# A fused four-layer kernel: new tables of the order in which side work is laid between the main pieces

## The chip, the cores and the metric

The kernel runs on one core of a Trainium2 chip. It has a matrix engine (TensorE, PE), a vector engine (VectorE, DVE), a scalar engine (ScalarE, ACT), a general engine (GpSimd, POOL) and a queue engine (SyncE, SP) that here issues the DMA transfers. Each works through its own list of instructions in order and meets the others through semaphores. The metric is the device time of one execution in microseconds; of several, the median.

## The reference

The input x is 8 images of 256 channels of 64 x 64 pixels, fp32. Four layers follow one another, each on the group-normalised value with a residual:

```python
def _gn(v, G=32, eps=1e-5): ...            # groups of 8 channels
# layer 0: three gates, mixed by weights from a 1-D convolution
b3 = x * sigmoid(bn(conv7x7([x.max(axis=1), x.mean(axis=1)])))
# b1, b2: the same with the channel axis swapped with H, with W
pooled = ((b1 + b2 + b3) / 3.0).mean(axis=(2, 3))
wts = softmax(conv1d(pooled, w1d), axis=1)
y0 = (wts * stack([b1, b2, b3])).sum(axis=1)
# layer 1: 3x3 convolution, 256 -> 256, with
w = a[0] * weight + sum(a[i + 1] * _cir_project(weight, b) for b in (2, 4, 8, 16))
# layer 2: the mean of a wavelet low band, then squeeze and excite
w = sigmoid(relu(mean(dwt2_ll(x)) @ W1.T) @ W2.T);  y2 = x * w
# layer 3: attention in shifted 8x8 windows, 8 heads
attn = softmax(q @ k.T * dh ** -0.5 + bias + mask);  y3 = (attn @ v) @ w_o + b_o
```

## The kernel before

**Main line.** One image after another goes through the same list of main pieces, FRONT: norm0a to norm0c (normalisation, with statistics gathered before), reduce0 to reduce15 (maxima and means over channels, transposed on PE), zpool, hwconv, hwgate, hwrows, band0 to band3, bandcopy, bandturn, hwmean0 to hwmean7 (the three 7x7 convolutions as products with band tables, and their gates), logits, mix, mixturn, gate0 to gate17 (layer 0's sum), norm1a to norm1c, lift0 to lift3 (normalisation and the transform of the convolution's input), conv0.0 to conv23.1 (24 accumulations in two halves, matmuls of 128x512) and convend. In the last image the attention remains to be done.

**Side streams.** Beside the main line each engine has streams of other work. A letter stands for the next step of a stream:

- POOL: R row sums over channels of the next image (lines 960 to 971), D differences and W weighed rows for layers 1 and 2, E the power in the excitation (line 910), N normalised probabilities (line 915), O heads (line 930), Y setup. Line 834 is the main line's power that gives the reciprocal root of a variance.
- DVE: C and U statistics and maxima of the next image (lines 1720, 1735, 1742), V row sums of layer 2 (lines 1706, 1709), B input transform, J the sums that join layer 1 to its residual, E excitation, K token remainders, S scores with bias and their maxima (lines 1836, 1847), T totals, A additions (line 1864), Y setup (line 1275 sums the circulant blocks of the weights). Line 1423 writes the convolution's input; line 1547 writes s, which PE needs before the bands.
- PE: Q a fill of qkv or output projection (lines 2141, 2148, 2157), S the score pairs (line 2173, tiles of 32 x 64), T turns (line 2183), W the products with the values (line 2201, tiles of 64 x 32), E, Y. S and W use small tiles; everything else uses the whole array.
- ACT: K token rows, Q evacuations of the fills (line 1189 writes vv), X exponentials, T, O, H, E, Y. Line 1080 writes g_raw for the reduces.
- SP: L loads and S stores of attention rows, Z stores of the image to scratch, F fetches of the next image, G the band tables again (its third transfer is line 681), Y setup.

The attention of image n thus runs beside the main line of image n + 1, and the statistics of image n + 1 beside the convolution of image n.

**Order.** Four tables set where each letter stands. FIRST is for image 0 and TURN for images 1 to 7: after the main piece that is the key, the letters of the value are played. AHEAD says how many letters of TURN have been played in image 0 already and are left out once, in image 1. LAST_ROWS is what follows after the last main piece. All engines read their own table; nothing else orders the steps. Per image the tables hold the same letters for SP (25), POOL (92), ACT (160), DVE (162) and PE (150).

## Time and profile before

| | us |
|---|---|
| median of 3 runs | 2744.55 |
| lowest and highest run | 2733.57, 2748.24 |
| profiled execution, span | 2740.3 |
| PE busy | 2332.0 |
| DVE busy | 2165.5 |
| ACT busy | 1538.2 |
| POOL busy | 1436.9 |
| a steady image (one of images 2 to 6), length | 310.7 |
| the same, PE busy and DVE busy | 285.56, 256.34 |
| from the last convolution matmul to the end | 211.0 |

The profiled execution lies between the runs. The busy times of the engines overlap, so their sum says nothing; what counts is where PE stands still and which engine it then waits for. A steady image repeats itself within about 3 us. A timeline row gives its start, its duration, engine, line, operation, what is written and read, a count, and in brackets the time for which the engine had nothing before it and whose result ended that.

### The profile page before, as it was taken

The numbers are of one execution on the slowest core, as the hardware profiler recorded it, in microseconds if no ns is written. First come the engines' busy times: TensorE is split into PE (matmuls) and PEld (weight loads), VectorE is DVE, ScalarE is ACT, GpSimd is POOL, SyncE is SP. The second block draws the span as 40 slices with busy tenths as digits, with TensorE's granted clock in tenths as the row PEclk, the third lists the DMA queues.
The fourth block names the chain that finished last, engine by engine and source line by source line (L and its number), as shares of the span: only waits on it lengthen the run. The fifth ranks groups of instructions, "written<-read, shape, count | busy, mean of one in ns | idle before, by whom it ended". The sixth has DMA issues, their size and how long they took to land.

```text
span 2740.3 us, 67622 instructions
## 1 busy us (share of the span) xinstructions
PE 2332.0 (85%) x27766; PEld 1395.9 (51%) x27766; DVE 2165.5 (79%) x3697; ACT 1538.2 (56%) x3566; POOL 1436.9 (52%) x1150
## 2 busy tenths in 40 slices
PE   0457738899899989899898989899898999899887
PEld 0433326455654556554664556555664556545454
DVE  6877957878887798878887798869887788867655
ACT  1222126654775566754775566754766567655665
POOL 3324562456734574465834575465834575465455
PEclk9878969999999999999999999999999989999999
DMA  5400400115111331115111241105110241101121
GB/s 155 127 3 16 158 19 18 32 47 171 33 33 47 98 105 33 33 35 174 40 33 39 83 128 33 32 32 161 57 33 25 79 146 33 33 32 57 54 63 41
DMA packets 125428, 176.20 MB, mean 64 GB/s; under 512 B 72496, under 2 KB 114240, under 8 KB 115520
## 3 DMA queue, kind: packets, MB, share of 16 engines
q1 hardware_dynamic: 125120, 171.88, 20.0%
q8 instruction: 220, 3.60, 0.5%
q14 instruction: 88, 0.72, 0.1%
HBM read 98.95 MB, written 72.86 MB: 63 GB/s over the span
## 4 chain that ended last, share of the span: by engine, by line
PE 54%; DVE 23%; ACT 8%; issue 6%; POOL 4%; DMA 2%; SPq 2%; DVEq 0%; POOLq 0%; ACTq 0%
PE F L2082 18%; PE QP L2141 9%; PE QP L2148 4%; PE SP L2173 4%; PE F L1979 3%; PE O L2201 3%; PE QP L2157 3%; PE PTR L2183 2%; PE F L1955 2%; DVE g_raw L1423 2%; DVE xs L1836 2%; DVE mx L1847 1%; ACT xs L1201 1%; POOL tmp L960 1%; DVE sums L1855 1%
## 5 line engine op out<-in xcount | busy, mean ns | idle before, releaser
L2082 PE MATMUL F<-g_raw,cw_hi 128*128 128x512 f16 x2304 | 701.1, 386 | 20.7 <-DVE g_raw L1423 6.5
L1201 ACT ACTIVATE xs<-xs,mx 128x64 f32<-128x64 f32 x1792 | 445.7, 334 | 123.8 <-DVE mx L1847 123.8
L915 POOL TENSOR_TENSOR xs<-xs,rec 128x512 f32<-128x512 f32 x256 | 287.9, 1136 | 432.5 <-DVE rec L1857 428.3
L2082 PE MATMUL F<-g_raw,cw_lo 128*128 128x512 f16 x1152 | 443.8, 385 | 0.0
L2082 PEld LDWEIGHTS F<-g_raw,cw_hi 128*128 128x128 f16 x2304 | 224.2, 99 | 286.5 <-issue 17.8
L1208 ACT ACTIVATE prt<-PTR 128x512 f32<-128x512 f32 x256 | 151.0, 590 | 216.8 <-PE PTR L2183 191.0
L900 POOL TENSOR_TENSOR tmp<-X,uw 128x512 f32<-128x512 f32 x128 | 165.3, 1303 | 164.0 <-DVE y L1709 83.0
L1836 DVE TENSOR_TENSOR xs<-SP,bias 128x1024 f32<-128x1024 f32 (+2 forms) x192 | 159.7, 859 | 100.0 <-issue 54.2
L1423 DVE SCALAR_TENSOR_TENSOR g_raw<-l0c,gn,g_raw 128x512 f16<-128x512 f32 x192 | 171.6, 936 | 72.2 <-ACT g_raw L1140 36.9
L930 POOL TENSOR_TENSOR ot_lo<-ot,ot_hi 128x512 f16<-128x512 f32 x128 | 149.1, 1187 | 145.8 <-ACT ot_hi L1222 132.7
L2141 PE MATMUL QP<-tok_hi,qkv_hi 128*128 128x512 f16 x470 | 180.1, 383 | 43.4 <-ACT qq L1182 17.3
L1855 DVE TENSOR_REDUCE sums<-xs 128x16 f32<-128x1024 f32 x128 | 155.2, 1212 | 72.2 <-ACT xs L1201 46.0
L1182 ACT ACTIVATE qq<-QP,q_bias,q_scale 128x512 f32<-128x512 f32 x118 | 91.6, 776 | 202.7 <-PE QP L2141 202.5
L1979 PE MATMUL F<-ident,g_raw 128*128 128x129 f32 x1024 | 153.1, 296 | 45.6 <-DVE Z L1528 22.7
L2082 PEld LDWEIGHTS F<-g_raw,cw_lo 128*128 128x128 f16 x1152 | 113.9, 99 | 142.2 <-issue 6.5
L2141 PE MATMUL QP<-tok_hi,qkv_lo 128*128 128x512 f16 x470 | 179.6, 382 | 0.0
L2141 PE MATMUL QP<-tok_lo,qkv_hi 128*128 128x512 f16 x470 | 179.3, 381 | 0.0
L2201 PE MATMUL O<-prt,vv 64*32 64x64 f32 x8192 | 162.0, 222 | 8.1 <-ACT prt L1208 7.5
L1979 PEld LDWEIGHTS F<-ident,g_raw 128*128 128x128 f32 x1024 | 135.0, 203 | 65.3 <-DVE Z L1528 33.5
L1847 DVE TENSOR_REDUCE mx<-xs 128x16 f32<-128x1024 f32 x128 | 156.2, 1220 | 14.4 <-DVE xs L1836 0.9
L2183 PE MATMUL PTR<-ident,xs 128*128 128x128 f32 x1024 | 158.7, 278 | 6.5 <-ACT prt L1208 4.2
L2173 PE MATMUL SP<-kk,qq 32*64 32x64 f32 x8192 | 155.1, 225 | 5.2 <-ACT kk L1185 4.2
(331 smaller groups left out, 5586.4 us busy)
## 6 DMA issues: line engine op xcount, KB each, us to landing
scratch_x<-X SPq DMA_DIRECT2D x32, 1024.0 KB, 5.8
...
l0c<-scratch_t SPq DMA_DIRECT2D x8, 576.0 KB, 13.7
```

The lines of the kernel that those rows point to most:

```text
L915: G.tensor_tensor(keyed(sc[:, u % 4, :]), keyed(sc[:, u % 4, :]), rec[:, u % 4, :].unsqueeze(2).to_broadcast([P, 8, TOK]), ALU.mult).then_ ...
L1201: last = S.activation(keys, keys, ACT.Exp, bias=mx[:, u % 4, i:i + 1])
L1423: V.scalar_tensor_tensor(vin[:, slot(half, comp), 1, t, :, 1:1 + W], rows_view(src[:, t, :]), g_r[:, t:t + 1], vin[:, slot(half, comp), 0, ...
L1836: return V.tensor_tensor(windows(sc[:, buf:buf + 2, :])[:, :, w0:w1_, :], windows(SP[:, :, :])[:, :, w0:w1_, :], bias[:, kind, :, :, :].re ...
L1847: V.tensor_reduce(mx[:, buf:buf + 2, :].rearrange("p a k -> p (a k)"), sc[:, buf:buf + 2, :].rearrange("p a (k m) -> p (a k) m", m=TOK), A ...
L1855: seq.link(V.tensor_reduce(both(sums), sc[:, buf:buf + 2, :].rearrange("p a (k m) -> p (a k) m", m=TOK), AX.X, ALU.add))
L1979: last = T.matmul(turned_pair(j)[:, t, :], Gn[:, t, P * j:P * j + P], ident_mean[:, :], start=True, stop=True)
L2082: last = T.matmul(F[:, n % 2, :], wgt[:, ci, C3 * comp + dx, P * co:P * co + P], win[which], start=(ci == 0 and dx == 0 and j == 0), stop= ...
L2141: last = T.matmul(out_bank, wgt[:, ci, P * oc:P * oc + P], tk[:, ci, :], start=(j == 0), stop=(j == 5))
L2173: last = T.matmul(SP[TOK * h2:TOK * h2 + TOK, hs, 256 * cg + TOK * w:256 * cg + TOK * w + TOK], qq[rows, cg, win], kk[rows, cg, win], star ...
L2183: last = T.transpose(PTR[:, P * b:P * b + P], sc[:, u % 4, P * b:P * b + P], ident[:, :])
L2201: last = T.matmul(O[DH * (h % 4):DH * (h % 4) + DH, par, cols:cols + TOK], vv[rows, pair, DH * h:DH * h + DH], prt[rows, u % 2, P * b + TO ...
```

## The change

The four tables are laid out anew; no other line is touched. All letters of an image are still played as often as before over the whole program; POOL plays fewer R and one E fewer in image 0 and so more of them in image 1, DVE two A more. SP's G for image 1 is played in image 0, as before; for a later image it is now played in that image's own norm0a, and no longer in the convolution ahead of it. Some entries, before and after (in the changed kernel every line behind the tables has a number lower by 3):

```diff
 FIRST = {
-    "SP": {"norm0a": "Y", "reduce9": "YY", "hwmean1": "Y", "hwmean7": "Z", "mix": "F", "gate7": "Z", "conv1.1": "F",
-        "conv3.1": "F", "conv6.1": "G", "conv12.0": "ZZ", "conv21.1": "F", "conv23.1": "L"},
...
+    "SP": {"load": "Y", "reduce4": "Y", "reduce12": "Y", "gate2": "YZ", "gate3": "Z", "gate7": "F", "gate16": "F",
+        "lift2": "F", "conv5.0": "Z", "conv9.1": "F", "conv13.1": "Z", "conv15.0": "L", "conv19.0": "G"},
...
-    "DVE": {"load": "CCUCYCCCYCCUCYCYUYYUCYUCCCCCYY", "norm0b": "UY", "norm0c": "YY", "reduce0": "Y",
...
+    "DVE": {"load": "CCYCCCCCCCCCUCCUCCYCYYYYYYY", "norm0b": "UYY", "norm0c": "YY", "reduce0": "Y", "reduce1": "Y",
...
-    "PE": {"reduce10": "YY", "hwconv": "Y", "hwmean0": "Y", "hwmean5": "Y", "gate5": "Y", "gate8": "Y",
...
+    "PE": {"zpool": "Y", "hwconv": "Y", "hwrows": "Y", "band1": "Y", "hwmean5": "Y", "gate1": "Y", "norm1b": "Y",
...
 TURN = {
...
-    "PE": {"norm0b": "Q", "norm0c": "QT", "reduce0": "TQ", "reduce1": "QW", "reduce3": "Q", "reduce4": "T",
...
-        "gate17": "QQQT", "norm1a": "QT", "lift0": "SWT", "lift1": "WQ", "lift3": "STWWQ", "conv0.1": "Q",
...
+    "PE": {"norm0c": "QQTQ", "reduce0": "T", "reduce2": "Q", "reduce3": "WW", "reduce4": "Q", "reduce5": "TQ",
...
+        "gate15": "QQQT", "norm1b": "W", "lift0": "T", "lift1": "QW", "lift2": "T", "lift3": "QSTWW",
+        "conv0.1": "SQQ", "conv1.0": "Q", "conv2.1": "T", "conv6.0": "Q", "conv6.1": "T", "conv7.0": "Q",
...
```

In DVE's table of TURN, "norm1c": "S" is gone and "conv4.0" is "KSB"; "norm0b": "ET", "norm0c": "AKKUA" become "norm0a": "E", "norm0b": "T", "norm0c": "AKKAU"; convend changes from JJJVVVVCVVVVVEECEECESCECESE to JJJVVVVVVVVVECECEECESECESE; conv12 to conv17 hold less and conv18.1 holds VVCSJUJCCCJVCSV. In PE's, "conv17.1" is QTWSQTWSWW. In SP's, G goes from conv6.0 to the next image's norm0a.

The first place is PE in a steady image, from lift3 to the convolution (lines 2082 and 2079 are the convolution's matmuls, F the accumulators, QP the fills' bank, SP and O the scores' and the products'). Before:

```order
L2173 MATMUL SP<-kk,qq 64x64 x32
L2183 MATMUL PTR<-ident,xs 128x128 x4
L2201 MATMUL O<-prt,vv 32x64 x32
L2148 MATMUL QP<-qkv_hi,tok_hi 128x256
L2148 MATMUL QP<-qkv_hi,tok_lo 128x256
L2148 MATMUL QP<-qkv_lo,tok_hi 128x256
...
L2082 MATMUL F<-g_raw,cw_hi 128x512 x2
L2082 MATMUL F<-g_raw,cw_lo 128x512
```

And after:

```order
L2170 MATMUL SP<-kk,qq 64x64 x32
L2180 MATMUL PTR<-ident,xs 128x128 x4
L2198 MATMUL O<-prt,vv 32x64 x32
L2079 MATMUL F<-g_raw,cw_hi 128x512 x2
L2079 MATMUL F<-g_raw,cw_lo 128x512
...
L2170 MATMUL SP<-kk,qq 64x64 x32
L2145 MATMUL QP<-qkv_hi,tok_hi 128x256
```

The fill that stood ahead of the first convolution matmuls, and a pair of scores with it, stand behind the first two halves.

The second place is DVE while image 0 is loaded (line 1275 before and 1272 after sum the weights' blocks; stats and Z are the image's statistics and maxima). Before, the stretch from the first statistics to norm0a:

```order
L1720 BN_STATS stats<-X 128x6 x2
L1735 TENSOR_REDUCE Z<-X 128x16
L1720 BN_STATS stats<-X 128x6
L1275 TENSOR_TENSOR cw_lo<-xs 128x128x9 x2
...
L1275 TENSOR_TENSOR cw_lo<-cw_lo,xs 128x2x63
L1735 TENSOR_REDUCE Z<-X 128x16
L1720 BN_STATS stats<-X 128x6 x5
L1275 TENSOR_TENSOR cw_lo<-cw_lo,xs 128x2x72 x2
...
L1399 BN_AGGR mv<-stats 128x2 x2
```

And after:

```order
L1717 BN_STATS stats<-X 128x6 x9
L1732 TENSOR_REDUCE Z<-X 128x16
...
L1272 TENSOR_TENSOR cw_lo<-xs 128x128x9 x2
...
L1272 TENSOR_TENSOR cw_lo<-cw_lo,xs 128x2x63
L1272 TENSOR_TENSOR cw_lo<-cw_lo,xs 128x2x72 x2
...
L1396 BN_AGGR mv<-stats 128x2 x2
```

Within the weights' sums no statistics or maxima are left; all of the statistics stand ahead of them.

The third place is POOL at the passage from image 0 to image 1 (tmp and Z are the row sums, part the excitation's operand, gn the normalisation's). Before:

```order
L960 TENSOR_TENSOR tmp<-X 128x512
L960 TENSOR_TENSOR tmp<-l0c 128x512
L910 TENSOR_TENSOR part<-part,neg_half 128x2
L960 TENSOR_TENSOR tmp<-tmp,X 128x512
L960 TENSOR_TENSOR tmp<-tmp,l0c 128x512
...
L971 TENSOR_TENSOR Z<-tmp 128x64
L974 MEMSET tmp 128x1024
L834 TENSOR_TENSOR gn<-gn,neg_half 128x2
```

And after:

```order
L957 TENSOR_TENSOR tmp<-X 128x512
L957 TENSOR_TENSOR tmp<-l0c 128x512
L907 TENSOR_TENSOR part<-part,neg_half 128x2
L831 TENSOR_TENSOR gn<-gn,neg_half 128x2
L912 TENSOR_TENSOR xs<-xs,rec 128x512 x2
L957 TENSOR_TENSOR tmp<-tmp,X 128x512
L957 TENSOR_TENSOR tmp<-tmp,l0c 128x512
```

The rest of the row sums now stands behind the reciprocal root of norm0.

## Rows read from the trace of the kernel before

**Rows 1.** The page: span, each engine's busy time, chain that ended last by engine.

```profile
span 2740.3 us, 67622 instructions
...
PE 2332.0 (85%) x27766; PEld 1395.9 (51%) x27766; DVE 2165.5 (79%) x3697; ACT 1538.2 (56%) x3566; POOL 1436.9 (52%) x1150
...
PE 54%; DVE 23%; ACT 8%; issue 6%; POOL 4%; DMA 2%; SPq 2%; DVEq 0%; POOLq 0%; ACTq 0%
```

**Rows 2.** Table of windows, steady image: length, busy (instructions) per engine, clock, DMA share, GB/s.

```profile
976.10:999.90 23.80, 17.31 (x338) 11.83 (x336) 20.96 (x57) 13.46 (x32) 16.75 (x13) 1.00 0.44 135
...
1138.30:1154.50 16.20, 12.04 (x304) 9.18 (x303) 12.84 (x22) 10.21 (x19) 4.84 (x4) 0.89 0.01 2
...
1219.00:1258.20 39.20, 39.20 (x378) 20.91 (x377) 33.17 (x41) 19.04 (x40) 17.48 (x13) 1.00 0.23 68
1258.20:1286.80 28.60, 27.42 (x191) 13.15 (x190) 27.21 (x41) 15.67 (x45) 16.46 (x14) 1.00 0.75 240
sum 310.70, PE 285.56 PEld 171.25 DVE 256.34 ACT 194.27 POOL 172.47; mean PE 25.96 PEld 15.57 DVE 23.30 ACT 17.66 POOL 15.68
```

**Rows 3.** Timeline of PE within a convolution: start, duration, line, operation, count.

```profile
889.78 0.65 PE L2201 MATMUL O<-prt,vv 64*32 64x64 f32 x32
890.36 0.66 PE L2183 MATMUL PTR<-ident,xs 128*128 128x128 f32 x4
...
903.45 0.99 PE L2201 MATMUL O<-prt,vv 64*32 64x64 f32 x64
904.37 0.61 PE L2082 MATMUL F<-g_raw,cw_hi 128*128 128x512 f16 x2
```

**Rows 4.** Timeline of all engines before the convolution (brackets: idle before, releaser).

```profile
1142.71 1.23 DVE L1836 TENSOR_TENSOR xs<-SP,bias 128x1024 f32<-128x1024 f32 x1 [0.55 <-PE SP L2173]
...
1144.04 1.22 DVE L1847 TENSOR_REDUCE mx<-xs 128x16 f32<-128x1024 f32 x1
...
1147.35 1.42 DVE L1423 SCALAR_TENSOR_TENSOR g_raw<-l0c,gn,g_raw 128x512 f16<-128x512 f32 x2 [0.95 <-ACT g_raw L1062]
...
1150.17 2.35 POOL L814 TENSOR_TENSOR l0c<-l0c 128x1024 f32<-128x1024 f32 x1 [7.27 <-DVE l0c L1409]
1150.95 2.78 DVE L1423 SCALAR_TENSOR_TENSOR g_raw<-l0c,gn,g_raw 128x512 f16<-128x512 f32 x2 [0.86 <-ACT g_raw L1062]
1151.37 0.57 ACT L1189 ACTIVATE vv<-QP 128x512 f32<-128x512 f32 x1
...
1151.99 0.39 PE L2148 MATMUL QP<-qkv_hi,tok_hi 128*128 128x256 f16 x1 [2.97 <-ACT vv L1189]
```

**Rows 5.** The page's group of the line that writes the convolution's input.

```profile
L1423 DVE SCALAR_TENSOR_TENSOR g_raw<-l0c,gn,g_raw 128x512 f16<-128x512 f32 x192 | 171.6, 936 | 72.2 <-ACT g_raw L1140 36.9
```

**Rows 6.** Timeline at the head of a steady image, ACT and PE.

```profile
1005.40 2.36 ACT L1080 ACTIVATE g_raw<-X,gn 128x1024 f32<-128x1024 f32 x2
...
1007.82 1.16 PE L1979 MATMUL F<-ident,g_raw 128*128 128x129 f32 x8 [0.85 <-ACT g_raw L1080]
```

**Rows 7.** Timeline of image 0, DVE during loading.

```profile
31.31 3.96 DVE L1275 TENSOR_TENSOR cw_lo<-xs 128x1152 f32<-128x1152 f32 x4 [11.19 <-DMA xs<-in_w_conv]
...
41.28 1.86 DVE L1742 TENSOR_REDUCE Z<-X 128x32 f32<-128x1024 f32 x1
...
53.81 3.06 DVE L1720 BATCH_NORM_STATS2 stats<-X 128x6 f32<-128x512 f32 x5
```

**Rows 8.** Timeline of image 0, PE in the reduces and before the band.

```profile
114.54 1.52 PE L1920 MATMUL SP<-ident,xs 128*128 128x128 f32 x6 [6.14 <-DMA xs<-scratch_w]
...
142.57 0.39 PE L2000 MATMUL F<-ident,s 128*32 128x128 f32 x1 [12.38 <-DVE s L1547]
```

**Rows 9.** Timeline of DVE between image 0 and image 1.

```profile
364.95 0.16 DVE L1767 SCALAR_TENSOR_TENSOR part<-F,part 128x2 f32<-128x2 f32 x1 [12.33 <-POOL part L910]
...
389.07 0.16 DVE L1450 SCALAR_TENSOR_TENSOR gn<-F,gn 128x2 f32<-128x2 f32 x1 [2.98 <-POOL gn L834]
```

**Rows 10.** Timeline of SP's queue in a steady image.

```profile
949.73 9.82 SPq L681 DMA_DIRECT2D l0c<-scratch_t  x1
```

More of the change, by code:

```diff
@@ L52 @@
 FIRST = {
[20 rows of a table removed]
-        "conv23.1": "UVV", "convend": "JJVJVCCVCVCVVCUVVVCEUUUCEEUECECUEUUEUUCCECUCE"},
-    "PE": {"reduce10": "YY", "hwconv": "Y", "hwmean0": "Y", "hwmean5": "Y", "gate5": "Y", "gate8": "Y",
-        "conv19.1": "Y", "conv23.1": "EEEEEE"},
[21 rows of a table added]
+        "convend": "JAJJCVVVVVVVVYUCUUEUCUEUCCCUUCEEECUCCECCACUEUUEE"},
+    "PE": {"zpool": "Y", "hwconv": "Y", "hwrows": "Y", "band1": "Y", "hwmean5": "Y", "gate1": "Y", "norm1b": "Y",
+        "conv1.0": "Y", "conv23.1": "EE", "convend": "EEEE"},
@@ L76 @@
 }
 TURN = {
[35 rows of a table removed]
-        "convend": "JJJVVVVCVVVVVEECEECESCECESE"},
[11 rows of a table removed]
-        "conv23.1": "TQTWWTQWQTEWE", "convend": "QEESEQSEQ"},
[14 rows of a table added]
+        "logits": "TQTX", "mix": "XQOQ", "mixturn": "KKX", "gate2": "T", "gate3": "K", "gate5": "KQXQT",
[16 rows of a table added]
+        "conv23.0": "VCK", "convend": "JJJVVVVVVVVVECECEECESECESE"},
+    "PE": {"norm0c": "QQTQ", "reduce0": "T", "reduce2": "Q", "reduce3": "WW", "reduce4": "Q", "reduce5": "TQ",
+        "reduce6": "ST", "reduce7": "WWSQ", "reduce8": "Q", "reduce10": "Q", "reduce13": "T", "reduce14": "Q",
+        "reduce15": "QTWQ", "hwconv": "QTWQT", "hwgate": "WQWS", "hwrows": "QSQ", "bandcopy": "Q", "bandturn": "T",
[8 rows of a table added]
+        "convend": "QTWTQTWWEWEQEESEQSEQ"},
@@ L127 @@
 }
-AHEAD = {"SP": {}, "POOL": {"R": 28, "E": 1, "N": 4, "O": 1}, "ACT": {"X": 2, "T": 4, "O": 1}, "DVE": {"U": 13, "E": 1, "T": 2, "A": 2}, "PE": {"Q": 2, "T": 4, "W": 4}}
+AHEAD = {"SP": {"G": 1}, "POOL": {"N": 4, "O": 1, "R": 22}, "ACT": {"O": 1, "T": 4, "X": 2}, "DVE": {"A": 4, "E": 1, "T": 2, "U": 13}, "PE": {"Q": 2, "T": 4, "W": 4}}
 LAST_ROWS = {
-    "SP": "LSLSLSLSLSLSLSSSL",
-    "POOL": "ENNNNXOXXNNXNXXNOXNNXNNXXONXXNNNXXXNOXNNNXXNOXNXNNXXOXNNXNNXXXOXNNNNXXXNXONNNO",
-    "ACT": ("KKXXQTQQKKTQTTXOKKXKQQQXQXTKTTTXOXKKKTXQXQTKQQTTOKXXKTXQXQQQKTTKXTXOXKKXQTQQQKTKTTXXOKTKQXXQTQKQTTOK"
-            "KXKXKXQQTXQQTKTXTXOKKKTQXXQQKQTTXTXXOTXTTTO"),
-    "DVE": "EATKAKTSSPPKKAATTSPSPTKAKATSSPKTKPAATSSTPPKAKATSTPPKSKAATSPSKAPKATTSSPPTKKAATSSTPTPAAASTA",
-    "PE": ("QQTQQQTQQWTSQTWSWWQQQQQQTTSWQQWTSTWWQQTQQQTQTWWSQTWWSQQQQTQQQTWSTTSWQWWQQQTQQQQTSTWWTQWWQSTQQWQQTQQW"
-            "TSWTSWQQQQQQQTQQTSTWWTSWWQQQQTQQTQWSTWTSWWQQTQQTWTWTWWQQ"),
+    "SP": "LSGLSLSLSLSLSLSSLS",
+    "POOL": "ENNNNOXXXNXNNNXXONXXNNNXOXXXNNNNXXONXXNNNXXONNXXNNXOXNXNXNNXXONXXNNNXXXNXNONNO",
+    "ACT": ("KKXXKQTKTQQQTTOKKXXQQQXXTQTKTKKTXXOKXTKXQQKTQQTTOKKXXXKQXQTQTQKTTOXXKKXQXTKKQQQTTTXOXKKTXXQQKTQQTTOX"
+          "KKKXQQXXTQQTKKTKTOKXXQQXXTQQTTKXTXOTXXKTTTO"),
+    "DVE": "EAKKATTSPSKPKAATTSKPTPSKAATSPSKPKAATTSSPTKPKAATSSPTKPKAATSSPPAKKTATSPKSPKTAATSSTPPTATAASA",
+    "PE": ("QQQQTQTQTWWSWTQWSQQQQQQQTQTSWTQWTWWSQQTQQQTQTWWSWTQWSQQQQQQTQTWWTSTWWSQQQQTQQQTQWSTWWTSWQQQQTQTQQQWW"
+          "TSTWWSQQQQQQQTQQTWSTQWTWWSQQQQTQQTSWTSTWQWWQTWTQWTQTWWQQ"),
```

115 rows, old and new, of tables (FIRST, TURN) are left out of this document.

## The prediction

> **What bounds the kernel now.** I read the page first. TensorE (PE) is busy for 85% of the span and is 54% of the chain that ended last; VectorE (DVE) is 79% busy and 23% of that chain; GpSimd (POOL) has 4% of it [rows 1]. So PE sets the time, DVE is next, and an edit counts only where PE stands still. The table of windows says where that is. A steady image takes 310.70 us with PE busy for 285.56 of it and DVE for 256.34 [rows 2], so PE idles 25.1 us an image. None of that lies in conv12 to conv17 (39.20 busy of 39.20). The 23.8 us between the last convolution matmul and the next norm0 hold 6.5 us of it, with DVE busy for 20.96 there, and the 16.2 us of norm1 and lift before the convolution hold 4.2, at a granted clock of 0.89 [rows 2]. The rest is small stops in the other stages. A shuffle inside the convolution is covered by PE; one at its two borders is not. Image 0 and the passage from image 0 to 1 have waits of their own, up to 12 us each [rows 7 to 9].
>
> The sum is made against the profiled span of 2740.3 us [rows 1], which is 4 us under the median of the runs; a saving in it is taken off the median, 2744.55, one to one.
>
> **Image 0.** Loading: DVE waits 11.19 us for the convolution's weights and then does, between its weight sums, seven pieces C and three U of the image's statistics [rows 7]. The new order puts the C in front of the wait, and of U two; the third goes behind norm0. Five C take 3.06 us, so seven take 4.3; U take 1.86, 1.86 and about 1.2, so 4.9. norm0 should begin 9.2 us earlier. PE then stops for 6.14 us inside the reduces, for a weight transfer needed by a setup step, and 12.38 us before the band, for DVE's s [rows 8]. The setup step moves behind the reduces, so the first stop goes. The second is a chain: s needs POOL's row sums, and these now stand 16 before the clearing of hwgate and 4 behind it, where there were 10 and 10. It can't give back more than the two waits and the load together less what DVE still owes: the setup pieces are not fewer, only later, and DVE is nearly the whole time busy here. From above 9.2 and a part of the 12.38, some 14; from below 0, if the weight chain, which has to be through before conv0, sets the end. I take 11, near the load term, since that is the one with an idle wait in front.
>
> **Image 0 to 1.** With no attention rows to fill it, this passage is a chain DVE, POOL, DVE. DVE idles 12.33 us for POOL's power in the excitation, and 2.98 us for POOL's rsqrt in norm0 [rows 9]. Before, POOL works at row sums in front of each. Now the last six of them stand behind the rsqrt: of the 2.98 some 0.7 is the operation itself, so 2.3 is gained. DVE's eight V, which release these row sums, are no longer mixed with five C and a U (3.1 + 1.2 by [rows 7]); an addition and one C now precede them (0.7 + 0.6), which leaves 3.0. Before the first power stands one row sum more (about 0.4 with its share of the small ones), before the second one fewer (1.3). -2.3 - 3.0 + 0.4 - 1.3 = -6.2; and the fetch that DVE waits for stands earlier on SP. From -2 (POOL's rate is the limit and the V gain nothing) to -10. I take **-6.2**.
>
> **A steady image, seven times.** Four edits lie outside the convolution's cover.
> - *norm1 and lift.* Before conv0, DVE has scores in its way (1.23 and 1.22) and PE has a fill that waits 2.97 us for ACT's vv, although conv0's own input was written by 1148.8 (1147.35 + 1.42) [rows 4]. After, one S and that fill are behind conv0, and DVE's S of norm1c is gone from there. Conv0 comes between 1.4 us earlier (what the letters take off DVE less what ACT puts back) and 5 (the whole wait and the slow restart of PE behind it). I take 2.5, most of the 2.97 that is seen, since the next convolution pieces need the second L1423, at 1150.95, too.
> - *norm0.* The first reduce waits 0.85 us for ACT's g_raw, two of 2.36 us together [rows 6]; a fill more stands before it on PE, which fills that wait, and an addition comes before a maximum on DVE. -0.8.
> - *The tail.* One C fewer (0.6) between the V. -0.6, or worse by up to 1 where the C placed behind the first E meets a fetch that is not down.
> - *Small and whole tiles.* A lone W begins 0.58 us before the next matmul; two in a row take 0.92, 0.46 each [rows 3]. So a change costs 0.12 us. I counted the changes in the new order: 481 against 530 in the program, 61 against 68 in each of these images. 7 x 0.12 = 0.8, of which I take 0.7, the changes in stages where PE waits anyway giving nothing.
>
> Against these stand a scores piece and a K more where PE already waits for DVE in the mix (+0.5), and the block that goes into conv18 and 19: DVE has about 6 us more in conv18 to conv22 and 7.5 less in conv12 to 17. I book +1.5 for its lateness, and price the bad case below. -2.5 - 0.8 - 0.6 - 0.7 + 0.5 + 1.5 = **-2.6** an image, seven times **-18**. From +2 (no gain at conv0, the block as booked) to -5.
>
> The port: line L1423 takes 1.42 us for two when alone and 2.78 beside POOL's L814 [rows 4]; DVE's maxima at 1.86 [rows 7] read from one place only and are not in that state. The Trainium skill (SBUF — State Buffer, section Who interferes with whom) says that a DVE operation with two SBUF inputs contends with a GpSimd one that reads SBUF, while a tensor_reduce never contends. By that rule a table that keeps POOL away from DVE gains on two-input lines alone, and if all of that counted the sum would be rival 4's. The trace agrees, with the 2.78. What all of L1423 loses is bounded by its group: 171.6 us for 192 [rows 5], against 192 x 0.71, is 35 us in the program, 4.4 an image. Nearly all of it lies in the convolution, where DVE has room (33.17 of 39.20 [rows 2]) and PE doesn't wait. So I book nothing for it; the one on the path, the 1.36 of [rows 4], still has L814 beside it.
>
> SP: the band tables' transfer, 9.82 us of SP's queue [rows 10], goes from the convolution to norm0 of the next image. There it delays a load of attention rows, not a fetch, and has the whole reduce stage until hwconv needs it; nothing booked.
>
> **The ending** has 8 tile changes or so fewer and otherwise the same latency-bound pattern: **-1**, from -6 to +5, since the order within it is a new one all through.
>
> **Sum.** -11 - 6.2 - 18 - 1 = -36.2: 2744.55 - 36.2 = **2708**.
>
> **The rivals.**
> 1. *The steady image doesn't move.* The convolution eats what is gained at its head, because DVE gets to conv18 no sooner and the tail is bound by DVE (20.96 of 23.8). For it: DVE is busy 256 of 310 and nothing is removed from it. Against: the 2.97 is a wait of PE. Then only -11 - 6.2 - 1 are left, and some of it: 2722 to 2735, about 2727. Chance 0.20.
> 2. *Slower: DVE is late at conv18 to conv23.* In these 28.60 us DVE is busy 27.21 [rows 2]. With 6 more it would need 33.3, 4.7 more than PE's own pace, and the accumulators' emptying would hold PE. It decides when the 6 us don't fit into the block of attention work that PE now has before conv18 (some 7.7 us of it by the durations of its letters). Seven images at 4.7, with the other gains of an image kept at 2, less image 0's and the passage's, is +19 - 18.2, about even; if the held PE also falls to the lower clock at the restart, as the fill at 1151.99 did [rows 4], 2.5 more each: +17. 2745 to 2775, **2762**. Chance 0.14.
> 3. *Image 0's gain is lost* to the weight chain: 2719. Chance 0.12.
> 4. *The ports count for more*: the shorter L1423 bring DVE sooner to the tail, 4.4 an image at most, half of it is -15: 2692, down to 2677. Chance 0.08.
>
> **How the numbers follow.** The forecast case (2695 to 2722) has 0.44; 0.02 is left for none of these. A measurement of this kernel tells about 0.5%, 13.7 us, from no change. Faster by more than that (under 2731): the forecast, rivals 3 and 4, and a third of rival 1: 0.44 + 0.12 + 0.08 + 0.06 = 0.70. Same: the rest of rival 1 and the even end of rival 2, 0.18. Slower: 0.12. The range is 2680 to 2748: it takes in the forecast, rivals 1 and 3 and most of 4, and leaves out most of rival 2.
>
> **What would show it.** Right: norm0 of image 0 some 9 us earlier, by the loading term; the stop of 6.14 us gone; POOL's rsqrt of image 1 directly behind a power; conv0 of a steady image 14 us instead of 16.2 after norm1's begin, with no wait for vv in front; some 308 us an image. Wrong: DVE waits for nothing in conv18 to 23 while PE waits for its gather (rival 2); the band's wait for s still over 10 us (rival 3); PE waits before hwconv for the tables.

## The result

| | us |
|---|---|
| before, median of 4 runs | 2742.92 |
| changed kernel, median of 4 runs | 2648.03 (2641.66 to 2652.97) |
| ratio, 95% interval | 0.9655 (0.9632 to 0.9679) |
| profiled execution of the changed kernel, span | 2651.2 |

The kernel is 3.45% faster, 95 us, where 36 were predicted: the direction was right, the size was 2.6 times too small, and the time lies below the predicted range.

The page of the changed kernel, the lines that answer to [rows 1]:

```profile
span 2651.2 us, 67608 instructions
...
PE 2304.1 (87%) x27766; PEld 1386.2 (52%) x27766; DVE 2186.5 (82%) x3697; ACT 1535.1 (58%) x3566; POOL 1441.2 (54%) x1150
...
PE 48%; DVE 17%; POOL 11%; ACT 7%; issue 5%; DMA 0%; DVEq 0%; SPq 0%; POOLq 0%; ACTq 0%
```

PE is busy for 28 us less and DVE for 21 us more. So DVE did not become quicker; it spends more time, in places where nobody waits for it. PE runs the same 27766 matmuls; the mean clock that it was granted over the execution goes from 0.951 to 0.961. So of the 89 us between the two spans 61 are idle time of PE and 28 are work that it did in less time. In the chain that ended last POOL goes from 4% to 11%.

The two profiled executions cut at the same eight borders (start to norm0, to conv0, to the last convolution matmul of image 0, to norm0 of image 1, to norm0 of image 2, to norm0 of image 7, to its last convolution matmul, to the end), in windows: length, busy time of PE, PEld, DVE, ACT and POOL, clock, DMA share, GB/s. Of before the sixth and the last:

```profile
689.20:2242.70 1553.50, 1434.24 (x17325) 859.34 (x17325) 1286.92 (x2175) 970.84 (x2342) 868.00 (x685) 0.97 0.21 66
...
2529.30:2740.30 211.00, 173.59 (x3162) 108.95 (x3160) 118.66 (x182) 131.44 (x233) 104.13 (x95) 0.97 0.18 54
```

And after, six of the eight:

```profile
52.40:202.90 150.50, 73.40 (x406) 53.91 (x407) 133.64 (x283) 41.02 (x75) 42.59 (x36) 0.80 0.22 60
202.90:309.50 106.60, 98.44 (x433) 42.45 (x434) 89.78 (x121) 22.58 (x35) 58.25 (x40) 0.97 0.17 60
309.50:355.40 45.90, 4.01 (x18) 3.11 (x16) 40.63 (x83) 0.56 (x2) 39.77 (x33) 0.55 0.46 149
355.40:654.00 298.60, 275.76 (x3297) 166.89 (x3297) 235.99 (x408) 185.20 (x444) 142.31 (x108) 0.97 0.16 51
654.00:2170.10 1516.10, 1415.89 (x17325) 851.85 (x17325) 1303.63 (x2175) 968.38 (x2341) 875.61 (x686) 0.98 0.22 68
...
2450.00:2651.20 201.20, 171.45 (x3162) 109.34 (x3160) 118.32 (x183) 130.55 (x232) 101.77 (x94) 0.98 0.18 54
```

| stretch | before | after | difference | predicted |
|---|---|---|---|---|
| start to conv0 of image 0 | 217.6 | 202.9 | -14.7 | -11 |
| convolution of image 0 | 112.8 | 106.6 | -6.2 | 0 |
| to norm0 of image 1 | 53.6 | 45.9 | -7.7 | -6.2 |
| seven images (305.2 + 1553.5 + 286.6 before) | 2145.3 | 2094.6 | -50.7 | -18 |
| the ending | 211.0 | 201.2 | -9.8 | -1 |
| sum | 2740.3 | 2651.2 | -89.1 | -36.2 |

The prediction's term for the passage reaches past the border at norm0, to the rsqrt behind it, which comes 2.1 us earlier after that border (5.07 and 2.93 us behind it, before and after): by its own borders the passage gained 9.8 and the seven images 48.6.

More than half of what was missed lies in the seven images. In them PE is busy for 22.0 us less (1978.8 and 1956.8) and idle for 28.7 less. One of them, beginning with the tail of the image ahead, stage by stage (the windows of after that answer to [rows 2], with norm0, the reduces, two stages from there to norm1, and the first convolution pieces). Of before, those that [rows 2] does not have:

```profile
999.90:1007.80 7.90, 5.46 (x20) 2.46 (x20) 6.44 (x20) 7.52 (x18) 5.63 (x7) 0.78 0.00 0
1007.80:1045.90 38.10, 35.28 (x466) 27.20 (x467) 34.13 (x58) 28.63 (x66) 33.19 (x30) 1.00 0.11 33
...
1072.50:1100.40 27.90, 25.14 (x364) 17.05 (x364) 23.00 (x65) 17.40 (x45) 6.60 (x6) 0.88 0.13 39
1100.40:1138.30 37.90, 33.71 (x409) 18.57 (x410) 35.18 (x54) 27.67 (x74) 18.32 (x14) 1.00 0.19 58
...
1154.50:1183.00 28.50, 28.37 (x127) 12.58 (x125) 18.24 (x25) 18.60 (x51) 15.96 (x11) 0.94 0.00 1
```

And after:

```profile
935.10:958.00 22.90, 17.13 (x339) 11.68 (x337) 20.75 (x55) 13.07 (x33) 15.83 (x12) 1.00 0.44 140
958.00:967.60 9.60, 8.04 (x26) 3.48 (x27) 7.00 (x21) 8.29 (x17) 9.13 (x11) 0.64 0.05 19
967.60:1003.30 35.70, 34.84 (x503) 28.02 (x502) 33.60 (x56) 28.23 (x66) 31.45 (x27) 1.00 0.42 130
...
1028.40:1056.80 28.40, 24.36 (x360) 16.51 (x361) 22.02 (x64) 16.47 (x44) 4.58 (x5) 0.88 0.13 38
1056.80:1094.00 37.20, 33.91 (x410) 18.20 (x409) 35.30 (x55) 28.47 (x75) 21.12 (x16) 1.00 0.19 59
1094.00:1104.10 10.10, 8.48 (x228) 6.39 (x226) 6.54 (x16) 6.04 (x12) 1.60 (x2) 1.00 0.01 2
1104.10:1135.00 30.90, 29.54 (x207) 14.00 (x200) 27.92 (x31) 21.13 (x54) 15.86 (x10) 1.00 0.12 35
...
1172.70:1211.10 38.40, 38.40 (x425) 20.36 (x423) 33.43 (x46) 16.50 (x40) 18.31 (x14) 1.00 0.34 111
1211.10:1238.40 27.30, 27.30 (x140) 12.83 (x133) 25.80 (x39) 15.68 (x43) 17.16 (x15) 1.00 0.25 78
sum 303.30, PE 283.48 PEld 170.58 DVE 260.13 ACT 193.62 POOL 174.71; mean PE 25.77 PEld 15.51 DVE 23.65 ACT 17.60 POOL 15.88
```

An image takes 303.3 us where it took 310.7. PE stands still for 19.8 us (303.30 - 283.48) instead of 25.1, and is busy for 2.1 less. Norm1 and lift fall from 16.2 to 10.1 us, with the clock at 1.00 and no longer at 0.89; the first six convolution pieces grow by 2.4, since a fill and a scores pair are now among them: 41.0 for both stages against 44.7. Of these 3.7 us only 1.3 are idle time; PE's busy time over both stages falls from 40.41 to 38.02, and its granted clock, 0.89 and 0.94 there before, is 1.00 in both. The rest is in small amounts: the reduces with norm0 45.3 against 46.0, conv18 to 23 27.3 against 28.6, the tail 22.9 against 23.8. The 28.6 holds a stop of 1.18 us of PE, for DVE's addition (line 1864), that the trace of before has in this one of the seven images only.

### The profile page after: what moved, and what is told of

Its sections match the earlier page's. It is cut to its first block, busy times and chain, and to the rows that moved or that the text cites. A ratio compares the mean times of both kernels' runs of the same rounds, so it can differ in the third digit from the quotient of the medians.

```text
span 2651.2 us, 67608 instructions
## 1 busy us (share of the span) xinstructions
PE 2304.1 (87%) x27766; PEld 1386.2 (52%) x27766; DVE 2186.5 (82%) x3697; ACT 1535.1 (58%) x3566; POOL 1441.2 (54%) x1150
## 4 chain that ended last, share of the span: by engine, by line
PE 48%; DVE 17%; POOL 11%; ACT 7%; issue 5%; DMA 0%; DVEq 0%; SPq 0%; POOLq 0%; ACTq 0%
PE F L2079 22%; PE QP L2138 6%; POOL tmp L957 5%; PE O L2198 3%; PE QP L2154 3%; PE SP L2170 3%; PE QP L2145 3%; PE PTR L2180 3%; ACT xs L1198 2%; DVE xs L1833 2%; DVE stats L1451 1%; POOL ot_lo L927 1%; DVE sums L1852 1%; POOL tmp L964 1%; DVE mx L1844 1%
## 5 line engine op out<-in xcount | busy, mean ns | idle before, releaser
L2079 PE MATMUL F<-g_raw,cw_hi 128*128 128x512 f16 x2304 | 693.5, 383 | 14.8 <-DVE X L1491 7.2
L1420 DVE SCALAR_TENSOR_TENSOR g_raw<-l0c,gn,g_raw 128x512 f16<-128x512 f32 x192 | 161.8, 885 | 59.0 <-ACT g_raw L1059 36.5
L2079 PEld LDWEIGHTS F<-g_raw,cw_lo 128*128 128x128 f16 x1152 | 112.8, 98 | 139.4 <-issue 1.4
L1182 ACT ACTIVATE kk<-QP,bq,gm 128x512 f32<-128x512 f32 x117 | 90.6, 774 | 161.3 <-PE QP L2138 161.3
```

What stands on the lines that cost most here:

```text
L2079: last = T.matmul(F[:, n % 2, :], wgt[:, ci, C3 * comp + dx, P * co:P * co + P], win[which], start=(ci == 0 and dx == 0 and j == 0), stop= ...
```

## The experiments

Three of them give each table alone, seven cut the one for images 1 to 7 into stretches or engines, and the others move single letters of it. All times are medians, with the ratio against the kernel before, measured beside it, and its 95% interval; the medians of before lay between 2742.5 and 2743.7.

### Each table alone

`e1_lastrows` takes the new LAST_ROWS, all else as before:

```diff
 LAST_ROWS = {
-    "POOL": "ENNNNXOXXNNXNXXNOXNNXNNXXONXXNNNXXXNOXNNNXXNOXNXNNXXOXNNXNNXXXOXNNNNXXXNXONNNO",
+    "POOL": "ENNNNOXXXNXNNNXXONXXNNNXOXXXNNNNXXONXXNNNXXONNXXNNXOXNXNXNNXXONXXNNNXXXNXNONNO",
...
```

> The kernel before with only the new LAST_ROWS (SP's string kept). The prediction's own term for the ending is -1 us: about 2742. The trace of the changed kernel has the stretch from the last convolution matmul to the end at 201.2 us against 211.0, so if the new order of the last rows does that by itself, -9.8: about 2733. A rival: the ending is shorter because the tail and the state in which it is entered are, then LAST_ROWS alone gives nothing.

Measured: 2735.47, ratio 0.9965 (0.9951 to 0.9978), -7.2. The ending's order is worth most of the 9.8 by itself; in this run's trace PE's last convolution matmul is 200.4 us from the end, as in the changed kernel, and in that of `e3_turns`, with the old LAST_ROWS, 213.3. The term was -1. `e2_firstimg` takes the new FIRST and AHEAD:

```diff
 FIRST = {
-    "DVE": {"load": "CCUCYCCCYCCUCYCYUYYUCYUCCCCCYY", "norm0b": "UY", "norm0c": "YY", "reduce0": "Y",
+    "DVE": {"load": "CCYCCCCCCCCCUCCUCCYCYYYYYYY", "norm0b": "UYY", "norm0c": "YY", "reduce0": "Y", "reduce1": "Y",
...
```

> The kernel before with only the new FIRST (and AHEAD, which belongs to it; TURN and LAST_ROWS as before). The prediction's terms: -11 for image 0 and -6.2 for the passage, so -17: about 2726. By the trace of the changed kernel norm0 of image 1 comes 28.6 us earlier (355.4 against 384.0), 6.2 of it in image 0's convolution, for which the prediction had nothing: about 2714. If the late row sums that are then left to image 1 cost it something, between the two.

Measured: 2714.31, ratio 0.9889 (0.9866 to 0.9913), -28.4: all that the trace showed up to norm0 of image 1. `e3_turns` takes the new TURN:

```diff
 TURN = {
-    "SP": {"reduce4": "L", "reduce8": "S", "hwconv": "L", "band1": "S", "band3": "L", "mix": "S", "gate3": "L",
+    "SP": {"norm0a": "G", "reduce7": "L", "reduce10": "SL", "band3": "S", "mix": "L", "gate5": "S", "norm1a": "L",
...
```

> The kernel before with only the new TURN (FIRST and LAST_ROWS as before; SP's extra G is accounted for in AHEAD and LAST_ROWS). The prediction's term is 7 x -2.6 = -18: 2725. By the traces a steady image takes 303.3 to 303.7 us against 310.4 to 312, so -7.3 x 7 = -51 for the seven images: about 2692. If less than -40, part of what the traces show there comes in from image 0 and is not TURN's.

Measured: 2688.79, ratio 0.9793 (0.9767 to 0.9818), -53.9. The three add up to -89.5 of the 95: the tables hardly depend on one another, and each earned, within some 3 us, what its stretch of the trace shows.

### One letter of the sum's largest term

`e4_onefill`, on the kernel before:

```diff
 TURN["PE"]
-    "lift3": "STWWQ", "conv0.1": "Q",
+    "lift3": "STWW", "conv0.1": "QQ",
```

> The kernel before with one letter moved in TURN: the fill that waits 2.97 us for vv goes from lift3 (ahead of conv0) to conv0.1, on PE alone. The prediction takes 2.5 of this for each of seven images: -17.5, 2725. If PE's restart at the lower clock goes too (the fill in 2.5 us instead of 1.3, and the first convolution matmuls), up to -5 each: -35, 2708. If DVE's path to the second L1423 is what conv0 waits for in truth, the wait only moves into the convolution: 0 to -5.

Measured: 2741.86, ratio 0.9996 (0.9984 to 1.0009): nothing. Its timeline, PE and ACT behind the first convolution matmuls:

```profile
1150.97 0.57 ACT L1189 ACTIVATE vv<-QP 128x512 f32<-128x512 f32 x1
...
1154.83 2.00 ACT L1201 ACTIVATE xs<-xs,mx 128x64 f32<-128x64 f32 x8
...
1156.74 0.57 ACT L1189 ACTIVATE vv<-QP 128x512 f32<-128x512 f32 x1
...
1157.37 0.61 PE L2157 MATMUL QP<-ot_hi,wo_hi 128*128 128x512 f16 x1 [3.38 <-ACT vv L1189]
```

Conv0 does start earlier, 10.7 us behind norm1 instead of 16.2, and PE no longer waits ahead of it. But the fill now finds its bank full behind conv0: PE waits 3.38 us there instead of 2.97 ahead ([rows 4]), for the next vv, which stands behind eight exponentials on ACT. Norm1 to conv5 takes 44.1 us against 44.7. DVE's chain to conv0's input is not shortened by this move either: in the trace of before its second line 1423 begins 10.0 us behind line 1443 of the same norm1 (1150.95 and 1140.95), with the scores of norm1c between them; in the changed kernel, where these are gone, 7.9 us.

`g1_fillvv` takes these exponentials away from it as well:

```diff
 TURN["ACT"]
-    "lift2": "XQK",
+    "lift2": "QXK",
```

> The kernel before with two letters moved: the fill from lift3 to conv0.1 on PE (as in e4_onefill, which gave 0) and ACT's second evacuation of lift2 ahead of the exponentials. In e4_onefill's trace PE's wait of 2.97 us for vv became one of 3.38 us behind conv0, with eight exponentials (2.0 us) in front of vv on ACT. If ACT's order was what ate the gain: -2.0 an image, -14: about 2729. If DVE's chain ahead of conv1 holds it: the wait moves on once more, 0 to -4.

Measured: 2739.76, ratio 0.9985 (0.9972 to 0.9999), -4.0. Two waits of PE in `g1_fillvv`'s timeline:

```profile
1152.51 0.39 PE L2157 MATMUL QP<-ot_hi,wo_hi 128*128 128x512 f16 x1 [1.48 <-ACT vv L1189]
...
1158.37 0.61 PE L2157 MATMUL QP<-ot_hi,wo_hi 128*128 128x512 f16 x1 [2.44 <-DVE xs L1864]
```

The wait for vv is down to 1.48 us, and behind it is one of 2.44 for DVE's addition, line 1864, that was not there before. `h1_fillvvadd` was to take this next one away too:

```diff
 TURN["DVE"]
-    "lift1": "S", "conv0.0": "A",
+    "lift1": "S", "lift3": "A",
```

> As g1_fillvv (fill behind conv0, vv ahead of the exponentials), and DVE's addition from conv0.0 to lift3. In g1_fillvv's trace the wait for vv fell from 3.38 to 1.48 us, and a new one of 2.44 us stood behind it, for this addition, which waited behind two L1423 and an L1413 on DVE. If it is the next in the row and no more stand behind it: -2.4 an image, -17: 2723. If the addition now holds DVE up ahead of the convolution's input, as it has to wait for the fill: 0 or slower.

Measured: 2740.57, ratio 0.9985 (0.9975 to 0.9996), with the 1.48 and the 2.44 us as they were. It tells nothing of the addition: on DVE no step of the main line lies between lift3 and conv0.0, so every engine has the instructions of `g1_fillvv` in the same order, and the run is a repeat of it (-3.0 beside -4.0). Whether the addition is the last in the row stays open. `g2_head` keeps `g1_fillvv`'s letter of ACT, leaves the addition and moves the scores pieces, as the new tables do:

```diff
 TURN["PE"]
-    "lift3": "STWWQ", "conv0.1": "Q",
+    "lift3": "TWW", "conv0.1": "SQQ",
 TURN["DVE"]
-    "norm1c": "S", "conv4.0": "A",
+    "conv4.0": "SA",
```

> As g1_fillvv, and the scores piece of norm1c on DVE and its pair on PE go behind conv0 too, as in the new tables. If these four moves are the whole of what the new tables do at the head of the convolution (norm1 to conv5 from 44.7 to 41.1 us): -25, 2718. If the ACT letters of norm1a to norm1c, which this leaves as they were, are needed as well: about as g1_fillvv.

Measured: 2759.98, ratio 1.0066 (1.0044 to 1.0087): 16 us slower. With the scores gone from norm1c, DVE waits 2.73 us for ACT to pad the rows (line 1047), which still stands behind two of ACT's turns, and the scores' time is missing further on: PE waits 1.86 us for them behind conv0, then 0.69 for vv and 1.97 for the addition. So these moves, which the new tables make too, are a loss while ACT's letters of norm1 and what follows up to conv5 stand as they did.

The same letter the other way round, `f5_undofill` on the changed kernel, and the one wait left there, `f4_vv`:

```diff
 TURN["PE"]
-    "lift3": "QSTWW", "conv0.1": "SQQ",
+    "lift3": "QSTWWQ", "conv0.1": "SQ",
```

> The changed kernel with one fill back ahead of conv0 (the prediction's largest single term undone, in the new surroundings). The prediction's -2.5 an image undone: +17, 2666. If in the new order of ACT and DVE the fill would find vv ready: only the wait that the traces show, 0 to +1 an image, 2648 to 2655.

Measured: 2676.78, ratio 0.9769 (0.9745 to 0.9794): 29 us slower than the changed kernel, 4.1 an image. PE's row ahead of conv0:

```profile
1112.46 0.40 PE L2148 MATMUL QP<-qkv_hi,tok_hi 128*128 128x256 f16 x1 [4.43 <-ACT vv L1189]
```

```diff
 TURN["PE"]
-    "conv0.1": "SQQ", "conv1.0": "Q",
+    "conv0.1": "SQ", "conv1.0": "QQ",
```

> The changed kernel with the last fill of conv0.1 (a projection that waits 1.11 us for vv behind the fill before it) one half later, in conv1.0. If a wait of PE is worth its length: -1.1 x 7 = -8 against the changed kernel: 2640. If it is passed on as the single fill's was: 0, 2648.

Measured: 2645.24, ratio 0.9648 (0.9633 to 0.9662), beside 0.9655 for the changed kernel: no difference that these runs can tell. So a letter that is worth 0 in one order is worth 29 us in the other. The 2.97 us of [rows 4] were a real wait, but others, nearly as late, stood behind it.

### Stretches of TURN

`e5_tomix` has the new TURN on norm0a to logits, `e6_mixtoconv` on mix to conv0.1, `e7_convon` on conv1.0 to convend, each with SP's old order; letters are balanced at the border.

```diff
 # e5_tomix, for POOL, ACT, DVE and PE
+    TURN[engine] = new[norm0a .. logits] + old[mix .. convend]
 # e6_mixtoconv
+    TURN[engine] = old[norm0a .. logits] + new[mix .. conv0.1] + old[conv1.0 .. convend]
 # e7_convon
+    TURN[engine] = old[norm0a .. conv0.1] + new[conv1.0 .. convend]
```

> The kernel before with the new TURN only for the pieces from norm0a to logits (POOL, ACT, DVE, PE; SP as before), from mix on the old one; the counts of letters agree at that border but for one O of POOL, left out once behind it. The theory that the gain is made where PE stood: by the stages of the two traces norm0 to logits takes 98.5 to 99.1 us against 100.5, so -1.4 to -2.4 an image: -10 to -17, about 2729. The prediction had -0.8 + 0.5 - 0.2 there, so -3. The rival, that a gain needs the whole table since each part only passes its wait on: 0.

> The kernel before with the new TURN only from mix to conv0.1 (gates, norm1, lift and the first convolution piece, with the fill, the scores on DVE and PE, and ACT's evacuations in their new places). By the traces gate0 to the last piece before conv6 takes 78.2 us against 82.6: -4.4 x 7 = -31: about 2712, if the ACT order ahead of conv0 is what the single fill lacked. The prediction had -2.5 x 7 = -17.5 here. If this part only passes the wait into the convolution as the single fill did: 0 to -5.

> The kernel before with the new TURN only from conv1.0 to convend. By the traces conv6 to the last matmul takes 103.4 us against 103.8 to 105, the tail 22.9 to 23.1 against 23.8: -1.1 to -2.3 an image: -8 to -16, about 2731. The prediction had -0.6 and +1.5 here, +6: 2749. If the rival of the prediction is right that DVE is late in conv18 to 23, slower than 2749.

Measured: 2732.12 (0.9964, 0.9952 to 0.9976), -10.6; 2752.80 (1.0029, 1.0014 to 1.0045), +10.1; 2736.60 (0.9977, 0.9967 to 0.9987), -6.1. The parts come to -6.6, while the four engines' new tables together, `e8_spturn`, give -38.4. In `e6_mixtoconv` norm1 and lift take 10.1 us as in the changed kernel, but conv0 to conv5 take 33.4 to 35.1 instead of 30.9, with a stop of 1.88 us for POOL's probabilities. `h2_mixtoconv7` carries the new order on to conv7.1:

```diff
 # h2_mixtoconv7
+    TURN[engine] = old[norm0a .. logits] + new[mix .. conv7.1] + old[conv8.0 .. convend]
```

> The new TURN from mix up to conv7.1 (e6_mixtoconv with conv1 to conv7 added; SP, and everything from conv8.0 on, as before). If the head of the convolution is one unit that reaches from norm1 to conv5: norm1 to conv5 near 41.1 us in the trace instead of 43.6 to 45.2, -3.6 x 7 = -25 against before: 2718, where the shorter piece was +10. If the head needs the rest of the convolution too, near 2740.

Measured: 2729.29, ratio 0.9949 (0.9933 to 0.9966), -14.3. Its trace has 41.0 us from norm1 to conv5 in every image, as the changed kernel: the head of the convolution is one unit from the gates to conv5. But of the 3.6 us an image won there 2.0 are left at its end; PE stands still for about 1 us more between the reduces and norm1, and the tail takes some 0.6 more. `f2_mixon` goes on to the end of the image, with SP's new order:

```diff
 # f2_mixon
+    TURN[engine] = old[norm0a .. logits] + new[mix .. convend];  TURN["SP"] = new
```

> The kernel before with the new TURN from mix to the end of the image and SP's new order; norm0 to logits as before. Alone, mix to conv0.1 was +10 and conv1.0 on was -6, SP some -10. If the gain ahead of the convolution needs the order of conv1 to conv5 as well (norm1 to conv5 41.1 us against 44.7, -3.6 an image), the parts together give -25 where apart they gave nothing: with SP's and the tail's share about 2700 (2695 to 2708). If the parts simply add: 2742.7 + 10 - 6 - 10 = 2737.

Measured: 2714.02, ratio 0.9902 (0.9887 to 0.9917), -28.5. The stretch that is missing here gave -10.6 alone, and gives -25 on top of this one (2714.0 to 2688.8).

### SP's order

`e8_spturn` has the new TURN on all engines but SP; `f1_sponly` on SP alone:

```diff
 TURN["SP"]
-    "conv6.0": "ZG",
+    "norm0a": "G",
...
```

> The kernel before with the new TURN on POOL, ACT, DVE and PE but SP's as before: what SP's order (the band tables in norm0 and not in the convolution, the fetches) is worth. Against e3_turns' 2689: the prediction booked nothing: the same within 3. If the band tables in front of the second fetch held the statistics back in the tail, this is slower, by 1 to 2 an image: 2696 to 2703.

> The kernel before with only SP's new TURN (band tables loaded in norm0 instead of within the convolution, fetches after them no longer). e3_turns against e8_spturn had 15 us for this on top of the other engines' new tables, and e8_spturn's trace has PE standing still in conv18 to conv23 for 4.68, 2.39 and 0.84 us with nothing awaited while the tables' transfer is issued. If that stop comes with the transfer whatever the other tables are: -8 to -15, 2728 to 2735. If the old order of the engines is spared (its own trace shows no such stop over 0.6 us): within 3 of before.

Measured: `e8_spturn` 2704.23 (0.9858, 0.9839 to 0.9877), so SP's order is worth 15 us on top of the others; `f1_sponly` 2740.53 (0.9994, 0.9985 to 1.0003), so alone it is worth nothing. In `e8_spturn` SP's queue and PE, near the end of a convolution:

```profile
932.60 9.39 SPq L681 DMA_DIRECT2D l0c<-scratch_t  x1
```

```profile
932.79 0.73 PE L2201 MATMUL O<-prt,vv 64*32 64x64 f32 x46
...
934.11 0.61 PE L2082 MATMUL F<-g_raw,cw_hi 128*128 128x512 f16 x2
939.40 0.38 PE L2082 MATMUL F<-g_raw,cw_lo 128*128 128x512 f16 x1 [4.68 <-issue]
```

PE stands still for 4.68 us between two matmuls of one accumulation, with no semaphore that it waited for, while the tables' transfer is being issued. Such stops are there in images 4 and 6 too, for 1.11 and 2.39 us and for 0.92 and 0.84, in image 1 for 0.30, and in `e7_convon` for 2.83, 2.40, 0.85 and less; conv18 to 23 take 33.7 us in image 2 where they take 27.3. Over the seven images conv12 to 23 are 12.6 us longer than in `e3_turns`, of the 13.5 between the two profiled spans: this is where SP's 15 us lie.

What PE lacked is its own instructions, and the traces show it. Beside the transfers, one DMA queue (named instruction on the page) brings 220 packets of 16 KB, as many as one for every 256 of PE's 56375 instructions (27766 matmuls, as many weight loads, 843 for its semaphores). All 13 such stops of 0.3 us or more in `e8_spturn` and `e7_convon` from image 1's convolution on fall on the same place of a block of 256 (PE's instruction 193 or 194 past a multiple of 256), and each ends 1.2 to 1.5 us after a packet has landed: the one of 4.68 us ended at 939.40, the packet at 937.96. In the run of 64-fold scores and products (QTWSQTWSWW) that stands just ahead of conv18 in the new order, PE goes through 256 instructions in some 4 us; two packets there start 3.7 us apart in `e3_turns`, and 6.1 to 7.9 apart in the images that stop, where the transfer runs beside them. An image has 7035 of PE's instructions, 27.5 packets, so the borders of the blocks meet the transfer alike in every second image only, and the stops over 0.3 us beside the transfer are all in images 2, 4 and 6. With the transfer in norm0 little is left of this: 0.56 us at the same matmul of image 2 in `e3_turns`, 0.35 in `f5_undofill`, none over 0.15 in a convolution of the changed kernel; nor has the kernel before any, in which PE takes 5.7 to 7.2 us for a block there.

### Port and tile changes

`g3_port`, on the changed kernel:

```diff
 TURN["POOL"]
-    "conv3.0": "DD", "conv4.0": "DD",
+    "conv4.0": "DD", "conv5.0": "DD",
```

> The changed kernel with POOL's differences D moved one to two convolution pieces later (DD at conv4.0 and conv5.0 for DD at conv3.0 and conv4.0). In its trace two DVE operations that read twice (0.86 us alone) take 1.70 and 2.83 beside them. If collisions in the convolution cost nothing since PE never waits for them, the time stays at 2648 within 4 although DVE is busy for some 2 to 5 us less an image. If the port is where the kernel's time is, -2 to -3 an image: 2630.

Measured: 2653.70, ratio 0.9678 (0.9654 to 0.9702). The line in question, as one group, before (line 1657), in the changed kernel (line 1654) and in `g3_port` (line 1657):

```profile
L1657 DVE SCALAR_TENSOR_TENSOR l0c<-X 128x512 f32<-128x512 f32 x32 | 20.6, 684 | 0.0
```

```profile
L1654 DVE SCALAR_TENSOR_TENSOR l0c<-X 128x512 f32<-128x512 f32 x32 | 47.8, 1532 | 0.0
```

```profile
L1657 DVE SCALAR_TENSOR_TENSOR l0c<-X 128x512 f32<-128x512 f32 x32 | 39.5, 1273 | 0.0
```

The new tables more than double this line, by 27 us of DVE in the program. Taking 8 us of that away gains nothing, so these 8 cost nothing; the other 19 were not tried. `g4_tiles`, on the changed kernel:

```diff
 TURN["PE"]
-    "conv9.0": "QWWS", "conv10.0": "QTWSW", "conv10.1": "T",
+    "conv9.0": "QWW", "conv9.1": "S", "conv10.0": "QTWS", "conv10.1": "WT",
-    "conv17.1": "QTWSQTWSWW", "conv18.1": "Q",
+    "conv17.1": "QTWSQTWS", "conv18.0": "W", "conv18.1": "WQ",
```

> The changed kernel with the groups of small-tile products taken apart at conv9, conv10, conv17 and conv18: 8 changes between small and whole tiles more in each of seven images, 56 in all, in a stretch where PE does not wait. At the prediction's 0.12 us a change: +6.7, 2655. If a change costs PE nothing: 2648. If a change costs more than the rows showed, or DVE gets its scores too late: over 2660.

Measured: 2663.56, ratio 0.9714 (0.9692 to 0.9736), +15.5. Not all of that is changes of tiles: conv6 to conv23 take 106.5 us against 103.4 (of these 3.1 us an image 2.2 are left in the whole), and two waits in there are new:

```profile
1167.82 0.66 PE L2183 MATMUL PTR<-ident,xs 128*128 128x128 f32 x4 [1.67 <-POOL xs L915]
...
1217.20 0.28 PE L2148 MATMUL QP<-qkv_hi,tok_hi 128*128 128x256 f16 x1 [0.78 <-ACT vv L1189]
```

3.1 - 1.67 - 0.78 leaves 0.65 us for 8 changes, 0.08 each, by a difference of small numbers that takes the two waits at their full length; the prediction's 0.12 is of that order. The prediction counted 530 and 481 changes; in the order in which PE ran its matmuls there are 514 and 470, 6 fewer in a steady image and 6 in the ending. These 44 are worth, as an estimate by the two prices, 4 to 5 of the 95 us.

## Why the prediction was right or wrong

**What bounds the kernel: right.** The chain is PE's still, and 61 of the 89 us came where PE stood, in image 0, the passage, the two borders of the convolution, the reduces, the gates and the ending. The other 28 us the prediction had no term for: PE's work itself took less time. From conv0 of image 1 to the last convolution matmul of image 7 it was granted the lower clock in 19 stretches before, 105.8 us in all, and in 12 after, 75.1 us. No run separates the clock from the changes of tiles in them.

**Image 0: right in its working, a term was missing.** norm0 came 9.5 us earlier (9.2 predicted): DVE, whose rows here answer to [rows 7], waits 5.58 us for the weights and not 11.19, and sums them without a break:

```profile
30.65 3.96 DVE L1272 TENSOR_TENSOR cw_lo<-xs 128x1152 f32<-128x1152 f32 x4 [5.58 <-DMA xs<-in_w_conv]
...
51.67 0.60 DVE L1396 BATCH_NORM_AGGREGATE mv<-stats 128x2 f32<-128x48 f32 x2
```

The stop of 6.14 us within the reduces is gone. The wait for s, [rows 8], is 11.30 us still:

```profile
127.81 0.40 PE L1997 MATMUL F<-ident,s 128*32 128x128 f32 x1 [11.30 <-DVE s L1544]
```

Conv0 came 14.7 us earlier, just over the upper end that was given (14), not the 11 that was taken. A wait for s over 10 us was to be the sign of the third rival; it stands, and the gain is there all the same (`e2_firstimg`), so that sign was badly chosen. The convolution of image 0 was booked at nothing. It has stops of its own, 11.8 us of them before and 8.2 after, and PE is busy in it for 2.5 less: "a shuffle inside the convolution is covered by PE" is true of a steady image and was carried over to this one, whose windows were not read for it.

**The passage: right, and short.** -9.8 for -6.2 by the term's own borders (-7.7 to norm0), near the -10 that was its bound. DVE's wait for the first power fell from 12.33 to 2.69 us, its wait for the rsqrt of norm0 from 2.98 to 0.80.

**The steady image: this step failed, -2.6 for about -7** (48.6 to 50.7 over seven; -7.4 in the one shown). By its terms:
- *norm1 and lift* were given -2.5, most of the wait that was seen. The stage with the six pieces behind it gained 3.6 to 3.7, and f5_undofill prices the letter at 4.1. The reason failed first: the sum priced one wait as if its length were its worth, and e4_onefill shows 0 for exactly that step: the next vv, the addition and the scores stood behind it and took its place. What paid is that the engines' letters moved together there, of which the working named DVE's and PE's and took ACT's as "what it puts back". The size failed next: of the 3.7 us 2.4 are PE's busy time, with the clock at 1.00 where it was 0.89 and 0.94. The working named this "slow restart" for its upper bound of 5 and left it out of the 2.5.
- *norm0* -0.8 (measured with the reduces -0.7), *the tail* -0.6 (measured -0.9) and *the mix* +0.5 (its stage 28.4 against 27.9): right. *The tile changes* -0.7: an estimate of -0.5 to -0.7 by the 6 fewer an image and the two prices.
- *The charge* of +1.5 for DVE's lateness was wrong: conv6 to 23 take 103.4 us against 103.8. The window of conv18 to 23 has PE busy for all of its 27.30 us. DVE's busy time did not move there either, as the count of letters had it, but is 33.43 for 33.17 in conv12 to 17 and 25.80 for 27.21 in conv18 to 23; it grew in conv0 to 5, from 18.24 to 27.92.
- *Nothing* was booked for "the rest is small stops in the other stages", 14.4 of the 25.1 us. By stages PE's idle time fell by 2.0 us in the reduces, by 0.9 in the gates and 0.9 in norm0, and grew by 1.3 in the stage of the mix and by 1.2 in conv0 to 5. So it is not one more term that was missed; a table that is laid out anew moves every stop a little.
- *SP* was booked at nothing, since its transfer delays no one that waits. It is worth 15 us on top of the other new tables, by stops of PE for its own instructions that the trace of before does not have: SP's new order gains nothing on the old one, it keeps the other tables from losing.

**The ending: wrong, -1 for -9.8** (-7.2 by e1_lastrows), outside the term's own range (-6 to +5) too. PE's stops in it fell, those over 0.6 us from 22.9 to 16.3. It was taken for "the same latency-bound pattern" and not worked out; 8.8 of the 52.9 us that the sum misses of the spans' difference are here.

**The port: right.** Nothing was booked, and g3_port shows nothing for 8 of the 27 us that DVE loses more on line 1654. DVE's collisions did not become fewer: counted in the timelines as what each line with two SBUF inputs takes beside POOL over its shortest, a steady image loses 0.8 us outside the convolution where it lost 2.4, and 12.7 inside it where it lost 6.5. Most of what left the outside did not move: the pair of line 1423 beside POOL's line 814 still takes 2.59 us for 2.78, as was foretold, and only stands behind conv0's start now that conv0 starts earlier. The Trainium skill (SBUF — State Buffer, Who interferes with whom) tells which pairs collide, and the 1532 ns of a two-input line beside POOL agrees; what it costs the kernel hangs on whose wait it lengthens, and these runs show none that it does.

**The rivals.** The first (the steady image doesn't move) and the second (DVE late) are refuted by e3_turns; the third (image 0's gain lost) by e2_firstimg. The fourth, that more than the sum is gained, had the right side at 0.08, but for the ports: line 1423, which it named, takes 9.8 us less in the program (171.6 and 161.8), and two-input lines as a whole lose more than before. No run takes line 1423's part by itself. No rival said that the sum was short because most terms were left out of it, and the low end, 2680, left no room for that.

## What stays open

The steady image's small stops are not told apart: to mix, the new order gives -10.6 alone and -25 with the rest, and no run says which letters make the difference. How much of PE's shorter busy time is clock and how much is changes of tiles was not separated. Why the packets with PE's instructions come later beside SP's transfer was not tried, nor the new order with its run of small matmuls moved away from the transfer. The gain of 6.2 us in image 0's convolution comes with FIRST (`e2_firstimg`); which of its letters make it was read nowhere.
